# Two transformer layers on one core: inverse square roots on GpSimd, one mask matmul per score bank, and re-measured planner costs

## The reference

```python
# layer 0, attention: a softmax over keys, added to x (no values are mixed)
kv  = ctx @ W_k.T + b_k                       # (4, 512, 128) -> (4, 512, 512)
sim = ((layernorm(x) @ kv) @ kv.T) * 512**-0.5
x   = x + softmax(layernorm(sim) * ln_gamma + ln_beta)
# layer 0, feed-forward: dense tanh-GELU branch and 8 experts, top 2
h   = layernorm(x)
dense = rms(gelu(rms(h) @ w_gate) * (rms(h) @ w_up) @ w_down)
moe   = rms(sum over the token's two experts of weight * expert(rms(h)))
x   = x + rms(dense + moe)
# layer 1, attention: 16 query heads on 4 key heads of width 32, rope, causal
q, k, v = rms(layernorm(x)), rms(ctx), ctx
scores  = where(causal, rope(q) @ rope(k).T / sqrt(32), -1e30)
x   = x + softmax(scores) @ v @ w_out.T
# layer 1, feed-forward: SiLU, hidden width 2048
x   = x + (silu(h @ w_gate.T) * (h @ w_up.T)) @ w_down.T    # h = layernorm(x)
```

## Time and profile before

| | before |
|---|---|
| median of 3 timed runs | 1782.6 us (1780.9 to 1784.31) |
| the profiled execution | 1781.71 us, span of the trace 1780.0 us |
| TensorE busy | 1655.6 us (93%), 9204 matmuls |
| VectorE busy | 1130.1 us (63%) |
| ScalarE busy | 820.1 us (46%) |
| GpSimd busy | 270.1 us (15%) |
| mean granted clock of TensorE | 0.965 of full speed |
| DMA | 410.05 MB, mean 230 GB/s |

### The profile page before, as it was taken

How to read it: one execution, slowest core, us unless ns; L and a number is a source line. 1 busy time by engine, 2 the same in 40 slices (tenths; PEclk the granted TensorE clock), 3 DMA queues, 4 the chain that set the end, 5 groups by cost and what they waited for, 6 DMA issues and landing times. The chain is left out here.

```text
span 1780.0 us, 27304 instructions
## 1 busy us (share of the span) xinstructions
PE 1655.6 (93%) x9204; PEld 1328.9 (75%) x9204; DVE 1130.1 (63%) x2748; ACT 820.1 (46%) x1803; POOL 270.1 (15%) x301
## 2 busy tenths in 40 slices
PE   3699999799999997999999999998999989999998
PEld 2587788688999985776767766876777667688887
DVE  5788877855776738965777754499565554543222
ACT  3566564244776732325666655332354463421110
POOL 1213221551222113210010100142100000000000
PEclk9599999899999998999999999999999979999999
DMA  3325569498899897879789863788963524345661
GB/s 108 118 95 166 200 229 341 170 339 321 299 359 347 269 344 243 286 262 360 270 280 342 294 238 98 284 303 313 296 216 90 160 72 178 101 161 178 209 217 59
DMA packets 135594, 410.05 MB, mean 230 GB/s; under 512 B 16032, under 2 KB 30752, under 8 KB 131744
## 3 DMA queue, kind: packets, MB, share of 16 engines
q1 hardware_dynamic: 123552, 368.98, 60.1%
q0 software_dynamic: 11904, 39.33, 6.6%
HBM read 303.92 MB, written 104.33 MB: 229 GB/s over the span
## 5 line engine op out<-in xcount | busy, mean ns | idle before, releaser
L1318 PE MATMUL ps<-xT,gu 128*128 128x512 f32 (+1 forms) x1224 | 453.3, 370 | 12.7 <-DVE gu L1834 5.6
L1320 PE MATMUL ps<-xT,gu 128*128 128x512 f32 (+1 forms) x1224 | 441.8, 361 | 0.0
L1319 PE MATMUL ps<-xT,gu 128*128 128x512 f32 (+1 forms) x1224 | 440.8, 360 | 0.0
L1318 PEld LDWEIGHTS ps<-xT,gu 128*128 128x128 f32 x1224 | 233.3, 191 | 49.6 <-issue 11.0
L1318 PE MATMUL ps<-wd,hid 128*128 128x512 f32 x604 | 247.9, 410 | 24.1 <-issue 11.4
L1320 PEld LDWEIGHTS ps<-xT,gu 128*128 128x128 f32 x1224 | 233.0, 190 | 35.3
L1319 PEld LDWEIGHTS ps<-xT,gu 128*128 128x128 f32 x1224 | 233.7, 191 | 29.4
L1319 PE MATMUL ps<-wd,hid 128*128 128x512 f32 x604 | 240.2, 398 | 0.0
L1320 PE MATMUL ps<-wd,hid 128*128 128x512 f32 x604 | 240.2, 398 | 0.0
L1531 ACT ACTIVATE hid<-act 128x512 fp32r<-128x512 f32 (+1 forms) x174 | 99.6, 573 | 246.4 <-DVE act L1819 245.8
L1819 DVE TENSOR_TENSOR act<-act,ps 128x512 f32<-128x512 f32 (+1 forms) x174 | 106.7, 613 | 148.3 <-PE ps L1320 147.8
(11 more groups left out here) (292 smaller groups left out, 2582.4 us busy)
## 6 DMA issues: line engine op xcount, KB each, us to landing
gu<-w_dram SPq DMA_DIRECT2D x150, 512.0 KB, 5.4
raw<-in_ffn_w SPq DMA_DIRECT2D x65, 768.0 KB, 6.0
wd<-w_dram SPq DMA_DIRECT2D x96, 512.0 KB, 5.2
w_dram<-raw SPq DMA_DIRECT2D x48, 512.0 KB, 4.8
gu_third<-w_dram SPq DMA_DIRECT2D x42, 512.0 KB, 3.8
w_dram<-gu SPq DMA_DIRECT2D x16, 1024.0 KB, 8.5
raw<-in_ffn_w POOLq DMA_DIRECT2D x48, 256.0 KB, 5.4
QT<-q_dram SPq DMA_DIRECT2D x48, 256.0 KB, 6.1
```

The source lines that it names most:

```text
L1318: mm(out_ap, ah, bh, start=start, stop=False)
L1319: mm(out_ap, ah, bl, start=False, stop=False)
L1320: return mm(out_ap, al, bh, start=False, stop=stop)
```

## The change

1. **Roots on GpSimd.** VectorE writes the variance (and, for the four `stats` kinds and `qnorm`, minus the mean) and signals `root_asked`; GpSimd raises it to the power -0.5 by one `tensor_tensor` with `pow` against a tile that holds -0.5, multiplies by minus the mean where there is one, and signals `rooted`, for which the readers wait. That is 41 powers and 24 multiplications on GpSimd, 24 more `tensor_scalar` on VectorE, and no more `inverse_root` there. `ROOT` is 1.
2. **Mask matmul.** For query tiles 0 and 1, 64 parts in all, the mask is added by one bf16 matmul per bank that covers both heads (128x2x128), the second head's score matmul no longer starts the bank anew, VectorE takes one minimum per part, and ScalarE reads PSUM and frees the bank.
3. **Durations.** Numbers in `steps` are changed, `SHARED` takes in GpSimd's roots, and `merge` gives another order on all engines.

```diff
-    ROOT = 3
+    ROOT = 1
+    ROOT_US = 1.3
     def masked_on_dve(n):
-        return True
+        return n // NG >= 2
-    SHARED |= {("POOL", kind) for kind in ("gam", "xh", "xt", "parts", "qsum", "kprep", "kscale", "qtab")}
+    SHARED |= {("POOL", kind) for kind in ("gam", "xh", "xt", "parts", "qsum", "kprep", "kscale", "qtab", "stats1", "simstats", "stats2", "stats4", "mnorm", "fnorm", "qnorm", "krs")}
         if kind == "rowt":
-            return [("PE", 0.36), ("ACT", 0.48)] + ([] if a[0] else [("DVE", 0.6)])
+            return [("PE", 0.42), ("ACT", 0.48)] + ([] if a[0] else [("DVE", 0.6)])
...
-            return [("DVE", (1.2 if kind == "stats1" else 0.6) if a[1] < n else 1.2 if a[1] == n else 0.6 if a[1] < n + ROOT - 1 else 1.0)]
+            return [("DVE", 1.2 if kind == "stats1" else 0.6)] if a[1] < n else [("DVE", 0.85), ("POOL", ROOT_US)]
...
-                        last = mm(..., start=True, stop=True)
+                        last = mm(..., start=at == 0, stop=True, skip_group_check=True)
```

On GpSimd:

```diff
+            def inverse_root(item, to, of):
+                pool.wait_ge(root_asked, ROOT_ASKED[item])
+                return tt(out=to, in0=of, in1=neg_half[:, 0:of.shape[-1]] if len(of.shape) == 2 else neg_half[:, 0:4].rearrange("p (a c) -> p a c", a=2), op=ALU.pow)
+            def row_scales(item, rs_, nm_, c=slice(0, TB)):
+                link(inverse_root(item, rs_[:, c], var_of[item[0]][:, c]))
+                tt(out=nm_[:, c], in0=neg_mean[item[0]][:, c], in1=rs_[:, c], op=ALU.mult).then_inc(rooted, 1)
```

On VectorE, `row_scales` ends with these two in place of the nine of `inverse_root` and L1788:

```diff
+                V_.tensor_scalar(var_of[kind][:, c], mv[kind][:, c, 1], mul, add, ALU.mult, ALU.add)
+                V_.tensor_scalar(neg_mean[kind][:, c], mv[kind][:, c, 0], -1.0, None, ALU.mult).then_inc(root_asked, 1)
```

More of the change, by code:

```diff
@@ L1210, in _ @@
             for kind, *a in ORDERS["POOL"]:
-                if kind == "gam":
+                if kind == "stats1":
+                    row_scales((kind, *a), rs1, nm1)
+                elif kind == "simstats":
+                    row_scales((kind, *a), rsim, nmsim)
+                elif kind == "stats2":
+                    row_scales((kind, *a), rs2, nm2)
+                elif kind == "stats4":
+                    row_scales((kind, *a), rs4, nm4)
+                elif kind == "qnorm":
+                    row_scales((kind, *a), rsq, nmq, slice(2 * a[1], 2 * a[1] + 2))
+                elif kind == "mnorm":
+                    c = slice(2 * a[1], 2 * a[1] + 2)
+                    inverse_root((kind, *a), rr[:, :, c], v2[:, :, c]).then_inc(rooted, 1)
+                elif kind == "fnorm":
+                    c = slice(2 * a[1], 2 * a[1] + 2)
+                    inverse_root((kind, *a), rf[:, c], var_of[kind][:, c]).then_inc(rooted, 1)
+                elif kind == "krs":
+                    inverse_root((kind, *a), krs[:, :], v16[:, :]).then_inc(rooted, 1)
+                elif kind == "gam":
                     b, i = a
@@ L1273, in _ @@
                 elif kind == "kscale":
-                    pool.wait_ge(k_scaled, 1)
+                    pool.wait_ge(rooted, ROOTED["krs", 0])
                     for b in range(B):
@@ L1463, in _ @@
                     for h, at in heads_of(n, p):
-                        last = mm(ps[:, 4 + p % 2, at:at + cols], QT[:, qt % 2, h, g, :], KT[:, g, 0:cols], start=True, stop=True)
+                        last = mm(ps[:, 4 + p % 2, at:at + cols], QT[:, qt % 2, h, g, :], KT[:, g, 0:cols], start=at == 0, stop=True, skip_group_check=True)
                     if not masked_on_dve(n):
@@ L1600, in _ @@
                         act_.wait_ge(xh_ready, nth("xh", *ROWS[m - 2][1:]))
-                    if k:
-                        act_.wait_ge(rows2_ready, b + 1)
-                    else:
-                        act_.wait_ge(rows_ready, b + 1)
+                    act_.wait_ge(rooted, ROOTED["stats2", b, TB] if k else ROOTED["stats1", b, 2])
                     shift, scale = (nm2, rs2) if k else (nm1, rs1)
@@ L2083, in _ @@
                     b, h, k = a
-                    if k == ROOT - 1:
-                        dve.wait_ge(u_ready, nth("qrow", b - 1, 2 * h + 1))
-                    row_scales(k, kind, 1.0 + RMS1_EPS, RMS1_EPS * LN_EPS, rsq, nmq, q_scaled, first=2 * h, n=2)
+                    dve.wait_ge(u_ready, nth("qrow", b - 1, 2 * h + 1))
+                    row_scales(kind, 1.0 + RMS1_EPS, RMS1_EPS * LN_EPS, first=2 * h, n=2)
                 elif kind == "qrow":
```

118 lines of the change are left out of this document (45 added, 73 removed).

## The result

| | before | after |
|---|---|---|
| median (4 runs each, same chip) | 1782.3 us | 1731.5 us (1728.8 to 1733.4) |
| ratio | | 0.970, interval 0.968 to 0.972 |
| span of the profiled execution | 1780.0 us | 1731.1 us |
| mean granted clock of TensorE | 0.965 | 0.978 |

The account below looks back on a forecast made before the run. The prediction took TensorE, busy 93% of the span, as the bound. Its eight terms, A to H, summed to -29.4 us against the 1780.0 us span, giving 1750.6 and a forecast median of 1753 us, range 1734 to 1784.

Parts of the forecast that it names:

- E: First combination of dense and expert results, 640 to 780 us: roots leaving VectorE save 9 us; ends -20 and +5.
- A: Mask matmuls: 64 added on TensorE, 0.118 us each, paid in full, cost 7.6 us; ends 0 and 15.1.
- B: The start, 0 to 81 us: shorter root chains, 0.9 us less each, save 3 us; ends -6 and +3.
- C: End of batch 2's attention, 1408 to 1447 us: new order fills gaps, saves 16 us; ends -18.6 and -8.
- D: Routing of tokens to experts, 320 to 341 us: more TensorE work beside it saves 6 us; ends -11 and +6.
- H: Rest of the new order, everywhere else: pieces stand differently and can only lose, +4 us; ends 0 and +15.
- F: Second combination, 1160 to 1250 us: 10 roots leaving VectorE save 3 us; ends -8 and +3.
- G: ScalarE table loads around layer 1's first feed-forward tile: 22 instead of 28, saves 4 us; ends -6 and 0.
- Rival 2: Late roots: GpSimd's power is long or queues behind wide products, deciding above about 3.5 us; 1788 us, chance 0.10.
- Rival 3: PSUM banks 4 and 5 held longer, through minimum and exponentials, so TensorE waits; 1768 to 1791 us, chance 0.12.
- Rival 4: Port shared by VectorE and GpSimd: moved roots hold its lock, halving E and F; 1759 us, chance 0.10.
- Rival 1: Order's gain only moves: gaps reopen elsewhere, C and D net nothing, H at upper end; 1779 us, chance 0.12.

## Why the prediction was right or wrong

**What bounds the kernel.** Right: the lost time stood where the earlier trace rows put it, and most of what was gained came from there. The split into two kinds of loss was right as well, and the runs now have a price for both: occupied VectorE cost 41 us, most of it in the combinations, and a longer way from engine to engine 0.8 to 1.0 us per us in the first attention and 0.3 to 0.4 behind it. Two terms, E and the one that is missing for 780 to 1120, fell short by 10.5 and 11 us; the others miss by 4 us or less each, and together take some 6 us back.

**A, masks, +7.6.** The price of one is right: in the changed kernel two scores and a mask start 0.36 us apart, 0.12 more than two scores did:

```profile
1346.14 0.48 PE L1501 MATMUL ps<-KT,QT 96*128 96x256 f32 x2
1346.46 0.28 PE L1504 MATMUL ps<-maskb,identb 128*128 128x256 bf16 x1
1346.50 0.48 PE L1501 MATMUL ps<-KT,QT 96*128 96x256 f32 x2
```

That the relief of VectorE counts for nothing was wrong: with the same order it pays for half of them or for all. By the medians the term nets 0, not +7.6.

**B, -3.** 2.1 were gained, but the way there had two errors that cancel: a power took 1.0 us, not 0.3, so the chain became 0.5 us shorter and not 0.9, and five roots lie in the stretch, not three or four. The forecast "powers under 0.5 us each" failed for every shape, and the one of 128x16 took more than the 2 us that I had named as a sign of being wrong; it is a single root, and the gain didn't hang on it.

**C, -16, and D, -6.** Right in size. C "is due to the order alone": in the order of the change, with the roots back on VectorE, less than 1 us is lost there, so it is. But which order the planner finds hangs on the roots: planned anew with roots on VectorE it left 19, 10 and 3 us, and with roots on GpSimd nothing each time. By what route the roots let the planner do so was not tried.

**E, -9: the step that failed.** I took "somewhat over a third" of VectorE's 24 us as TensorE's gain, because VectorE was 76% busy. VectorE got 20 us back there (107.0 to 87.2), and the stretch gave 19.5. With the order kept, the roots back on VectorE added 20 us to its busy time in the stretch and made it 16 us longer for the same matmuls; its occupied time alone added 18 and 13. So 0.7 to 0.8 of VectorE's relief reach TensorE, not a third. A stretch of 140 us at 76% is not evenly at 76%: TensorE lost its time in just the pieces in which VectorE had a full queue (6.15 us at 669, 5.47 at 704, by the timeline). The rest of the 19.5 came with the new order.

**780 to 1120: no term.** I gave the attention behind the combination only the table loads, -4, and it gained 15. In the kept order neither masks (1 us of lost time from 760 to 1085) nor roots (4 us) account for that much; by elimination the other 10 are the new order, whose attention stands in other places. I had allowed the new order only to lose ("can there only lose", H, +4), and left out a stretch with 22.1 us of loss spread thin, in which it could gain. This is the second step that failed, as large as E. Where a new order could lose, H was too low by 3.6: 9.5 us more are lost ahead of the first combination, 4.4 of them before the routing, and 2 less elsewhere.

**F, -3.** The second combination kept its loss (-0.3), though in the kept order the roots are worth 17 us in it (1079 to 1196). So the new order lost there what the roots gained; why was not tried.

**G, -4.** 22 table loads instead of 28, as counted; their price by itself was not tried.

**Rival 2, late roots.** Half of it came about. A power is short, 0.76 to 1.29 us on the mean of its shapes up to 128x4, but roots do stand behind wide products in GpSimd's list: 8 of the 24 in the combinations came after more than 3.5 us. That undid nothing, so "decides above about 3.5 us from request to result" was wrong for single roots. It was wrong for their sum as well: with 2.1 us of work added to each, the first twelve came at 4.4 us, the others at 5.8, and the gain was gone. The reader distance in the combination was counted, that in the first attention, where no other work hides a root, was not. By that run, a power of 3 us would have made this change worthless.

**Rival 3, banks held longer,** had no effect: the weight loads of the score matmuls waited 4.5 us in all, and the kernel with VectorE's masks is not faster. **Rival 4, the shared port,** hardly: VectorE's products of two SBUF tiles (`hid`) took 0.68 to 0.69 us beside powers, as without, where no wide product of GpSimd ran too. What the overlap cost fell on the power: six of the eight of 128x4 in the combinations took 1.21 to 1.54 us, against 1.00 to 1.03 for eleven of the twelve of the first attention. Wide products are another matter, as the earlier trace rows showed. **Rival 1** is refuted by the table of lost time: C's 18.6 us turned up nowhere else, except for 4 to 5 us each ahead of the routing and behind it. Its sum had an error: H at its upper end is 11 us more than in the forecast, not 7, which puts the rival at +4 and not at 0.

**The range.** It was built from independent ends of the terms, and its low side took E's -20 and C's -18.6 as rare. The gain of a change that acts through a planner has one common cause, and its terms go together; that is an argument, and one result can't show it.

## What to carry to other kernels

Relieving an engine that is busy for 63% of the time can still be worth much to the one that is the bound: read what it does in the gaps, not its mean. To price it, keep the planned order and bring one cost back: that shows what an occupied queue costs (41 us here), which a new plan mixes with 10 us or more of its own. Then look in the trace how long the way to the reader has become on either side, before a run with an artificial delay is read as a part of the gain: here the sum of the ways was nearly the same, 105.5 and 100.9 us. Measure the new operation before such a move: 2 us more a root would have undone all of it.

## What the runs showed of the hardware

A power on GpSimd took 0.70 to 0.74 us for most of 128x2, 1.00 to 1.03 for most of 128x4, and 2.90 for 128x16: about 0.5 us and 0.15 more per column, so my bound by the 1.28 us of a 128x512 product was no bound on a power; at 16 columns it is already double. The Trainium skill ("GPSIMD Engine Reference", section 3.1) gives 2.6 cycles an element for a two-input operation; a column of a power is far above that here (0.15 us, where a column of the 128x512 product took 1.28 / 512 = 0.0025), and the page has no power. A product of 128x4 beside it took 0.20 us. A hand-over between VectorE, GpSimd and ScalarE took 0.04 to 0.10 us in the chains at 12 and 32 us. Beside powers alone, VectorE's products of 128x512 kept their 0.68 to 0.69 us, and powers of 128x4 beside such work took up to 1.54.
